# State scan of a hybrid layer stack: step-size sum of the later units on POOL, its positive part on ScalarE

## The reference

```python
xc = silu(conv(x_e))                              # b, l, 256
delta = jax.nn.softplus(delta_r @ W_dt + b_dt)    # the step size
deltaA = jnp.exp(delta[..., None] * A[None, None])
deltaB_x = delta[..., None] * Bmat[:, :, None, :] * xc[..., None]
_, H = lax.associative_scan(combine, (deltaA, deltaB_x), axis=1)
y = jnp.einsum('bldn,bln->bld', H, Cmat) + xc * D[None, None, :]
y = y * silu(z)
return y @ W_out
```

## Time and profile before

| | |
|---|---|
| runs | 1981.05, 1990.20, 1988.71 us; median 1988.71 |
| span of the profiled execution | 1883.9 us (no whole time of that execution is recorded; the three runs are 97.2 to 106.3 us above the span) |
| busy in the span | PE 1376.5, DVE 1286.4, POOL 866.1, ACT 833.7 us |
| items of the scan | 1103.4 to 1594.1 us of the span |
| DVE busy there | scans 292.7, multiplications by B 154.8, step-size sums 17.8 us |
| POOL's products L2340 | 128, 302.5 us |
| granted TensorE clock | 0.84 of full, mean over the span |

### The profile page before, as it was taken

One profiled execution on the slowest core, in us unless ns is written; L12 is line 12 of the kernel. 1 busy time (PEld: TensorE's weight loads), 2 busy tenths in 40 slices (PEclk: granted clock), 3 DMA queues, 4 the chain that ended last, 5 costly groups with the idle time before them and its releaser, 6 DMA issues. The chain is left out here.

```text
span 1883.9 us, 29315 instructions
## 1 busy us (share of the span) xinstructions
PE 1376.5 (73%) x8975; PEld 714.5 (38%) x8976; DVE 1286.4 (68%) x2984; ACT 833.7 (44%) x1181; POOL 866.1 (46%) x763
## 2 busy tenths in 40 slices
PE   4459999999999798683995857586666544592992
PEld 2113333333333576552894322132221101362991
DVE  4568898988884255673332179999999998671433
ACT  3405666666667211121453458457475232121551
POOL 3401111121211434375565237867868665573662
PEclk9658999999999688797997778798788766796996
DMA  4721111211141566442333286985867763723335
GB/s 129 243 80 51 43 62 38 61 45 52 51 71 37 81 93 96 134 105 87 83 91 93 60 227 152 244 198 150 223 151 193 190 153 78 181 92 110 92 91 150
DMA packets 219597, 214.96 MB, mean 114 GB/s; under 512 B 49504, under 2 KB 188739, under 8 KB 217155
## 3 DMA queue, kind: packets, MB, share of 16 engines
q1 hardware_dynamic: 197454, 184.90, 39.5%
q0 software_dynamic: 9216, 19.02, 3.2%
q10 hardware_dynamic: 12800, 9.46, 1.7%
HBM read 149.46 MB, written 63.37 MB: 113 GB/s over the span
## 5 line engine op out<-in xcount | busy, mean ns | idle before, releaser
L806 ACT ACTIVATE attn_prob<-attn_ps_cols 128x1024 f32<-128x1024 f32 (+1 forms) x320 | 290.5, 940 | 224.1 <-PE attn_ps_cols L682 222.7
L2340 POOL TENSOR_TENSOR ssm_hc<-ssm_h,ssm_cb 128x1024 f32<-128x1024 f32 x128 | 302.5, 2364 | 169.2 <-DVE ssm_h L2323 124.4
L2323 DVE TENSOR_TENSOR_SCAN ssm_h<-ssm_decay,ssm_ps_u 128x1024 f32<-128x1024 f32 x128 | 292.7, 2287 | 17.6 <-DVE ssm_ps_u L2318 0.5
L832 POOL TENSOR_SCALAR_AFFINE_SELECT attn_prob<-attn_prob 128x512 f32<-128x512 f32 x128 | 81.2, 634 | 421.4 <-ACT attn_prob L806 421.3
L714 DVE CUSTOM_DVE_ANT_0 attn_ps_rows<-attn_ps_rows,const_mask_rows 128x384 f32<-128x384 f32 (+3 forms) x512 | 235.5, 528 | 39.6 <-PE attn_ps_rows L649 39.6
L649 PE MATMUL attn_ps_rows<-attn_ks,attn_qs 72*128 72x512 bf16 (+3 forms) x768 | 225.7, 346 | 42.7 <-DMA attn_qs<-parts_dram 29.2
L2311 ACT ACTIVATE ssm_decay<-ssm_wide,ssm_aneg 128x1024 f32<-128x1024 f32 x128 | 146.0, 1146 | 181.5 <-DVE ssm_h L2323 121.0
L2274 PE MATMUL ssm_ps_u<-ssm_stack,ssm_spread 96*128 96x512 bf16 x256 | 96.2, 465 | 177.3 <-DVE ssm_h L2323 172.3
L682 PE MATMUL attn_ps_cols<-attn_qs,attn_ks 75*128 75x512 bf16 (+3 forms) x768 | 191.8, 330 | 4.8 <-DMA attn_qs<-attn_nrows 4.0
L701 PE MATMUL attn_ps_o<-attn_prob,attn_vw 128*32 128x512 f32 (+3 forms) x1536 | 164.3, 500 | 0.3 <-POOL attn_prob L832 0.3
L719 DVE TENSOR_REDUCE attn_nm<-attn_ps_rows 128x1 f32<-128x512 f32 x256 | 157.6, 684 | 5.8 <-PE attn_ps_rows L649 5.8
(11 more groups left out here) (331 smaller groups left out, 2473.1 us busy)
## 6 DMA issues: line engine op xcount, KB each, us to landing
ssm_wide<-delta_dram SPq DMA_DIRECT2D x128, 512.0 KB, 6.6
attn_ks<-parts_dram SPq DMA_DIRECT2D x48, 192.0 KB
attn_qs<-parts_dram SPq DMA_DIRECT2D x48, 192.0 KB
parts_dram<-proj_parts SPq DMA_DIRECT2D x8, 768.0 KB, 3.8
ffn1e_x<-ex_dram SPq DMA_DIRECT2D x40, 130.0 KB, 2.3
ffn2e_x<-ex_dram SPq DMA_DIRECT2D x40, 130.0 KB, 2.3
split_dram<-ssm_parts SPq DMA_DIRECT2D x6, 768.0 KB, 4.3
ssm_stack<-split_dram SPq DMA_DIRECT2D x18, 256.0 KB, 4.2
```

The lines of the kernel that those rows point to most:

```text
L806: nc.scalar.activation(prob[u % RING][:, heads[0]:heads[-1] + 1, 0:w], ps_cols[s % 2][:].rearrange("p b (x q) -> p (b x) q", x=len(heads) ...
L2323: nc.vector.tensor_tensor_scan(h[t % H_RING][:], decay[t % DECAY_RING][:], ps_u[t % 2][:], 0.0, ALU.mult, ALU.add).then_inc(scan_done, 1)
L2340: nc.gpsimd.tensor_tensor(hc[:, t % HC_RING, :], h[t % H_RING][:], cb[b % 2][:], ALU.mult).then_inc(hc_done, 1)
```

## The change

Units 0 and 1 stay as they are. For units 2 to 7:

- ACT, between exp and ln, replaces v by its positive part, in place (a new step `relu`, with a semaphore of its own).
- POOL adds the two halves of `work` into `delta`, as a plain addition of two tensors. The step stands at s = 13 ahead of `u` for the even unit, and at s = 18 for the odd one. It takes over the waits that DVE had (the logarithm, the earlier unit's `u`, the earlier unit's store), and one for the positive part.
- DVE has neither step any more, and no wait for them.

```diff
-... 12: [("z0", 1), ("z1", 1), ("abs", 0), ("exp", 0), ("ln", 0)],
-... 17: [("middle", 0), ("abs", 1), ("exp", 1), ("ln", 1)],
+... 12: [("z0", 1), ("z1", 1), ("abs", 0), ("exp", 0), ("relu", 0), ("ln", 0)],
+... 17: [("middle", 0), ("abs", 1), ("exp", 1), ("relu", 1), ("ln", 1)],
...
-DVE_AT = {2: [("finish", 1), ("stats", 1)], 4: [("out", 0)], 5: [("out", 1)], 13: [("delta", 0)], 18: [("finish", 0), ("delta", 1)],
+DVE_AT = {2: [("finish", 1), ("stats", 1)], 4: [("out", 0)], 5: [("out", 1)], 18: [("finish", 0)],
...
-POOL_AT = {0: [("sum", 1)], 2: [("rstd", 1)], 13: [("u", 0)], 15: [("rest", 0)], 17: [("low", 0)], 19: [("u", 1)], 21: [("rest", 1)],
+POOL_AT = {0: [("sum", 1)], 2: [("rstd", 1)], 13: [("delta", 0), ("u", 0)], 15: [("rest", 0)], 17: [("low", 0)], 18: [("delta", 1)], 19: [("u", 1)], 21: [("rest", 1)],
...
+            if part == "relu":
+                act.wait_ge(abs_ready, did(n))
+                nc.scalar.activation(dtx_of(n)[:, at], dtx_of(n)[:, at], ACT.Relu).then_inc(relu_ready, 1)
+                return
...
                 dve.wait_ge(ln_ready, did(n, ch))
-                if n >= 2:
-                    dve.wait_ge(u_ready, did(n - 1))
-                    dve.wait_ge(delta_stored[1 - k], ((n - 1) // 2 + 1) * 16)
-                    dve.wait_ge(delta_begun[0], 16)
...
+        def make_delta(pool, n):
+            pool.wait_ge(relu_ready, n - 1)
+            pool.wait_ge(ln_ready, did(n))
+            pool.wait_ge(u_ready, did(n - 1))
+            pool.wait_ge(delta_stored[1 - n % 2], ((n - 1) // 2 + 1) * 16)
+            pool.wait_ge(delta_begun[0], 16)
+            pool.sem_inc(passed, 1)
+            nc.gpsimd.tensor_tensor(delta[:], dtx_of(n), soft_of(n), ALU.add).then_inc(delta_ready, 1)
```

More of the change, by code:

```diff
@@ L1926 @@
 ACT_AT = {0: [("conv0", 0)], 2: [("conv1", 0)], 4: [("norm", 1)], 6: [("z0", 0), ("z1", 0), ("turn", 1)], 7: [("silu", 0), ("conv0", 1)],
-          8: [("conv1", 1)], 10: [("dr", 0)], 11: [("dt0", 0), ("dt1", 0)], 12: [("z0", 1), ("z1", 1), ("abs", 0), ("exp", 0), ("ln", 0)],
-          13: [("silu", 1)], 15: [("high", 0), ("dr", 1)], 16: [("dt0", 1), ("dt1", 1)], 17: [("middle", 0), ("abs", 1), ("exp", 1), ("ln", 1)],
+          8: [("conv1", 1)], 10: [("dr", 0)], 11: [("dt0", 0), ("dt1", 0)], 12: [("z0", 1), ("z1", 1), ("abs", 0), ("exp", 0), ("relu", 0), ("ln", 0)],
+          13: [("silu", 1)], 15: [("high", 0), ("dr", 1)], 16: [("dt0", 1), ("dt1", 1)], 17: [("middle", 0), ("abs", 1), ("exp", 1), ("relu", 1), ("ln", 1)],
           18: [("b", 0)], 19: [("c", 0)], 20: [("b", 1)], 21: [("high", 1)], 22: [("c", 1)], 23: [("middle", 1)], 29: [("norm", 2)],
           30: [("turn", 2)]}
-DVE_AT = {2: [("finish", 1), ("stats", 1)], 4: [("out", 0)], 5: [("out", 1)], 13: [("delta", 0)], 18: [("finish", 0), ("delta", 1)],
+DVE_AT = {2: [("finish", 1), ("stats", 1)], 4: [("out", 0)], 5: [("out", 1)], 18: [("finish", 0)],
           27: [("stats", 2)]}
-POOL_AT = {0: [("sum", 1)], 2: [("rstd", 1)], 13: [("u", 0)], 15: [("rest", 0)], 17: [("low", 0)], 19: [("u", 1)], 21: [("rest", 1)],
+POOL_AT = {0: [("sum", 1)], 2: [("rstd", 1)], 13: [("delta", 0), ("u", 0)], 15: [("rest", 0)], 17: [("low", 0)], 18: [("delta", 1)], 19: [("u", 1)], 21: [("rest", 1)],
            23: [("low", 1)], 25: [("sum", 2)], 27: [("rstd", 2)]}
@@ L2018, in scan @@
         xn_ready, bank_done, bank_kept, gated_ready = (m.sem(n) for n in ("xn", "bank_done", "bank_kept", "gated"))
-        abs_ready, exp_ready, ln_ready, delta_ready, u_ready = (m.sem(n) for n in ("abs", "exp", "ln", "delta", "u"))
+        abs_ready, relu_ready, exp_ready, ln_ready, delta_ready, u_ready = (m.sem(n) for n in ("abs", "relu", "exp", "ln", "delta", "u"))
         delta_stored, split_stored, stacked = m.pair("delta_st"), m.pair("split_st"), m.pair("stacked")
@@ L2253, in prepare_pool @@
                 make_rstd(pool, n)
+            elif part == "delta":
+                make_delta(pool, n)
             elif part == "u":
```

## The result

The changed kernel took 1980.49 us (median of 20 runs, 1968.71 to 1991.16), the kernel before beside it on the same chips 1992.09 us (20 runs, 1979.32 to 2002.14): ratio **0.9952**, 95% interval 0.993 to 0.9974, that is 9.6 us gained, between 5 and 14. (The two medians are 11.6 us apart, which lies inside that interval; the text goes by the ratio.) The forecast was 10.4 us and 1978.3 us. The sum came out close; by batches it did not, and this is what the rest is about.

What follows compares the result with a forecast made beforehand. VectorE was taken to set the scan's pace at 3.54 us an item; of 18.9 us removable, waits at items 16 and 24 left 10.4 us, so 1988.7 − 10.4 = 1978.3 us, range 1968 to 1986.

Steps and rivals of the forecast that it cites:

- The sum: Batch gains of 2.6, 3.4 and 4.4 us in the scan, together 10.4 us, giving 1978.3 us; chance 0.63.
- What is removed: Six step-size sums and their waits leave VectorE in the scan: at most 18.9 us gained.
- The remaining 24 us: Rest of VectorE's time in the scan stretch, taken as finishing, statistics and residual work.
- ScalarE at item 16: Added positive part delays the decay, so VectorE waits 1.0 to 1.1 us before item 16's scan.
- The odd store 25.3 us after item 13's product: POOL runs without pause from item 13, so the odd unit's step-size store comes 25.3 us after that multiplication starts.
- Item 24: Its decay follows the odd store by 13.4, 14.8 and 13.7 us; VectorE waits there, 4.6 us in all.
- faster: Whole-time outcome beyond the 9.9 us a measurement can tell from no change; chance 0.51, against 0.43 for the same.
- Time around the span: Whole times of three runs lie 97 to 106 us above the profiled span; the median, 104.8, was kept.
- Supply keeps up: Rival: transfers or POOL come sooner, leaving only ScalarE's wait at item 16: 15.0 us gained, 1973.7 us; chance 0.18.
- POOL falls behind: Rival: POOL's operations stretch to 3.42 us in its unbroken run, making item 24 late: 21.7 us lost, 2010.4; chance 0.06.
- Mutual exclusion against VectorE: Rival: the sums on POOL hold up VectorE, 13.9 us back, 1983.7 us; chance 0.13.

Runs made afterwards that it cites:

- Run 1: Changed kernel with the sync queue issuing item 24's wide load ahead of the three stack loads: 1983.62 us, ratio 0.9959 to the kernel before.
- run 2: Control: kernel before the change, with item 24's wide load issued ahead of the three stack loads: 2000.85 us (one run), scan stretch 489.6 us.
- run 4: Kernel before, its six fused sums kept on VectorE but one item later (14 and 19): 1975.94 us (one run); repeated and timed, 1976.27 us, ratio 0.9953.
- runs of 8: Kernel before with sums at items 14 and 19 and item 24's wide load first: 0.9927; the same with VectorE's statistics at item 28: 0.9934.
- runs 2 and 3: The second of the pair: kernel before with the positive part on ScalarE and a plain addition on VectorE at items 13 and 18: 1983.68 us (one run).

## Why the prediction was right, and where not

- **What is removed.** The term of at most 18.9 us held: 10.84 + 7.84 = 18.7 us were gained at items 14 and 19, the sixth sum with 1.1 as stated. (The remaining 24 us of the stretch are not finishing, statistics and residual work alone: VectorE stood idle 17.6 us before scans and 5.9 before multiplications. No term rests on it.)
- **ScalarE at item 16**, forecast at about 1.1 us: measured 1.12 in the first and third batch. It failed in the second, where ScalarE's chain was itself late: 3.23 us, and 1.49 for TensorE at item 18. The step took ScalarE's gaps from one second batch before, where the gate multiplications had run at 1.88 us. I had not looked whether TensorE's clock there was full by luck.
- **The odd store 25.3 us after item 13's product**: 25.41, 28.35, 25.40. Right where POOL runs without a pause. The error is the assumption that it always does.
- **Item 24.** Chain of 13.4, 14.8 and 13.7 us, measured 13.2, 15.0 and 13.5. The waits, 4.6 us in all by forecast, came to 4.5, with the decay as the late one. Run 1 shows the queue order as the reason. In the second batch the agreement (2.1 us, forecast 2.4) is luck: VectorE arrived 3.6 us later than forecast, for the waits at items 15, 16 and 18, and the store came 3.0 us later than 25.3.
- **The sum.** 2.6, 3.4, 4.4 against 2.6, 0.2, 4.5: the second batch was mis-sized by 3.2 us, and the scan stage became 7.0 us shorter in the profiles, not 10. That the whole time came within 1 us of the forecast is in part chance: the trace of before held the cheap outcome of the tie in the first batch (run 2), and an execution with the dear one has 2.2 us more to give back. The forecast had priced neither that nor the low clock; they pull opposite ways. By the prediction's own bound of 9.9 us the gain, 9.6, falls just short of "faster", which it had given the larger chance (0.51 against 0.43); the interval keeps it clear of nothing gained.
- **Time around the span.** "The three runs lie 97 to 106 us above it, and I keep that" was a wrong reading, without effect on the difference. After has 1.8 us around its span. What is missing lies in the expert stages, below.
- **The rivals.** Supply keeps up: fell, item 24 waited. POOL falls behind: fell; its products have a longest of 2.40 us, none of 3.42. Mutual exclusion against VectorE: fell for scans (2287 ns as before), and held for the two operations with two SBUF inputs that were measured beside POOL, the fused sum and the plain addition, which is why the change helps. The Trainium skill's warning that offloading between the two "might not help" (Perfetto Trace Analysis, Optimizing Scalar/DVE Operations) did not decide here, 9.6 us being gained; but run 4 and its repetition give it a point: the offload itself earned nothing that a shift by one item did not.

## What to carry to other kernels

When an operation takes three times its own length, look at the engine beside it before moving the work: here the cost was a collision with POOL, and shifting the sum by one item on VectorE, to where POOL is done or VectorE starts first (two numbers, no new semaphore, no work for ScalarE or POOL), gave 0.9953 against the move's 0.9952. Before trusting one profile's slack, look at the same place in all its repetitions and ask which engine's clock or start could have fallen the other way; a chain that fits only at the full clock gives back a part of a batch's gain whenever the clock is low, here 1.7 to 3.6 us of a batch's 3.4 or 4.4. The gate multiplications were slow in 14 of the 24 batches behind the first. And count the places that are tight next (16, 24, 28 here) before pricing a gain: each of them could be cleared alone, and each time a smaller one came up.

## What the runs showed of the hardware that was not expected

**A tie of 0.01 us decides over 2.2 us**, shown in run 2: one cheap outcome in six.

**The same program took 100 us less on one chip.** Beside the two runs of 8 the kernel before took 1890.33 us (12 runs); beside all others its median was 1988.72 to 1992.09. The traces before and after show the same gap. The loop of the router over its eight tiles (VectorE's line 1382) takes 60.9 and 61.3 us in the two expert stages before, and 91.9 and 94.4 after. From the first to the last multiplication of the experts' first product are 113.6 and 113.9 us before, and 135.5 and 136.5 after. Together that is 108 us; other places differ by a few us either way. TensorE by line, the expert stage's first product (busy us, mean ns, idle before), in the trace before:

```profile
L1789 PE MATMUL ffn1e_ps_h<-ffn1e_xT,ffn1e_w 128*128 128x256 f32 x320 | 77.2, 385 | 0.9 <-ACT ffn1e_xT L1826 0.9
```

after:

```profile
L1789 PE MATMUL ffn1e_ps_h<-ffn1e_xT,ffn1e_w 128*128 128x256 f32 x320 | 79.1, 391 | 18.1 <-ACT ffn1e_xT L1826 17.0 <-issue 1.0
```

and in the last run of 8, on the quick chip:

```profile
L1789 PE MATMUL ffn1e_ps_h<-ffn1e_xT,ffn1e_w 128*128 128x256 f32 x320 | 77.1, 384 | 0.9 <-ACT ffn1e_xT L1826 0.9
```

The runs 2 and 3, which leave the expert stages and (run 2) everything but one load as before, show waits of 17.5 to 18.3 us on this line, and both runs of 8 show 0.9; so the wait goes with the chip and not with the kernel. The profile of before thus looks like one from a chip of the quick kind, and its three runs like ones from the other. What makes the two kinds differ was not tried. The scan's stretch is the same on both (476.0 to 478.7 us for the kernels of runs 4 and 8), which is why it served as the measure.
